# Layer 0 of a four-layer forward pass: row sums of the attention weights spread by transfers instead of a product, and a new written-out order on all engines

## The chip, the cores and the metric

One core of a Trainium2 chip runs the whole program in one launch. The metric is device microseconds from start to end, lower is better. TensorE (PE), VectorE (DVE), ScalarE (ACT), GpSimd (POOL) and SyncE (SP, which here only issues transfers) each run their own list of instructions in order and wait on semaphores for one another.

## The reference

Four layers, each an attention-like branch and a feed-forward branch. Only the first layer is changed. Its two branches are independent up to the end of the part that is spoken of here:

```python
# branch 1: 8 blocks over x of 4 x 512 rows, width 128 (two rows of x share one sum over the sequence)
q, k, v = x @ Wq + bq, x @ Wk + bk, x @ Wv + bv
Q, K = elu(q) + 1, elu(k) + 1
KV, Ksum = (K * v).sum(seq), K.sum(seq)
V = Q * KV / (Q * Ksum + eps)
x = layernorm(gelu(V @ Wo + bo) + x)
x = layernorm(gelu(gelu(x @ Wf1 + bf1) @ Wf2 + bf2) + x)

# branch 2: attention with 16 heads of width 8
scores = q @ k.T / sqrt(8)
attn = softmax(scores)
o = attn @ v
return o @ wo.T + bo      # then norm and a mixture of experts
```

## The kernel before

The function `layer_0_branches` runs both branches at once.

Branch 1 is four streams of 512 columns (`s` = 0 to 3), each through eight blocks `i`. A block of a stream is 16 products of a 128x128 weight with 128x512 data in f32 (`q k v o`, the norm's `n1centre n1var`, `f0` to `f3`, four for `ff`, `n2centre n2var`), with ScalarE, VectorE and GpSimd steps between them. On PE all of them are line L110.

Branch 2 is 16 chunks `m`: half of 1024 queries for a group of four heads. Within a chunk:
- `search` (L498, 16 units of two bf16 products) gives the scores with queries on the rows; VectorE takes row maxima (`maximum`, L708), 2.44 us of it for two units.
- `negate`, `turn` (L507, one transpose on PE), `turn_copy` (L722), and four small transfers on SP (L427, `maxima_rows`) put the negated maxima into an extra row of the query stack.
- `weigh` (L523, 16 units) gives the scores turned, less the maximum; ScalarE takes Exp into `weights` (`weight`, L622).
- `use` (L540, 8 tiles of keys, each four heads side by side on the columns) adds weights times values into one bank, `out`. Row 32j+8 of it is the sum of head j's weights.
- `out` (L629) copies the bank to `mixed`; `sums` (L551, `add_up`) multiplies by the matrix `spread`, which brings row 32j+8 to all 32 rows of head j; `log` and `inverse` (L638, L642) take Ln and then Exp(-x) into the one tile `inv`; `divide` on GpSimd (L744) multiplies `mixed` by it.

The units of `search` and `weigh` share two double banks of PSUM in the order planned (`doubles`); the products of branch 1, `turn` and `sums` share three banks (`singles`). Chunk `m` searches while chunk `m-1` weighs. ScalarE must load another function table whenever it goes from Exp/Ln to Gelu (L566) or back (L561).

The order of the work on each engine is set by `in_order`, which merges the generators by the times that they yield. These times come from a table for one period of 44 units that is repeated 16 times: a time plus `PERIOD` times the chunk's (or block's) number. So the order is the same in each of the inner chunks.

When the last chunk is divided, a barrier of all engines ends the function, and the next one begins with the product of `mixed` with `wout`.

Of the kernel before, what the change touches and what calls it, by code (L numbers as in the profile page):

```python
# [8 lines left out]
ALU = mybir.AluOpType  # L9
ACT = mybir.ActivationFunctionType  # L10
# [217 lines left out]
class Ring:  # L228
# [27 lines left out]
PERIOD = 44.0  # L256
PLAN_ATT = {
    "q": (3.88, 0.80), "k": (-0.00, -3.02), "v": (5.37, 1.59), "exp_k": (0.98, -1.86), "relu_k": (1.52, -0.11),
    "exp_q": (6.24, 2.05), "relu_q": (6.77, 4.58), "less_k": (3.19, -1.17), "K": (4.35, 0.58), "less_q": (13.24, 11.61),
# [4 lines left out]
PLAN_NET = {  # L264
# [5 lines left out]
PLAN_CHUNK = {  # L270
    "search": (10.34, 14.80, 15.01, 18.78, 18.99, 22.65, 22.86, 29.45, 31.73, 36.64, 37.86, 39.71, 42.80, 48.77, 51.26, 54.14),
    "maximum": (12.12, 15.22, 17.08, 19.20, 20.26, 23.42, 24.48, 29.86, 32.17, 37.06, 38.27, 40.77, 43.22, 49.19, 51.67, 54.55),
    "negate": (55.92,), "turn": (59.40,), "turn_copy": (60.83,),
    "weigh": (69.73, 69.93, 72.01, 73.22, 75.52, 76.94, 78.15, 78.36, 80.43, 82.23, 83.50, 86.59, 90.48, 90.68, 92.98, 95.05),
    "weight": (70.77, 71.62, 72.46, 73.92, 75.93, 77.36, 78.57, 79.42, 80.85, 82.71, 84.04, 87.01, 90.89, 91.74, 93.39, 95.46),
    "use": (76.01, 77.23, 80.93, 84.00, 87.09, 90.97, 95.55, 116.29), "out": (117.36,), "sums": (129.64,), "log": (132.28,),
    "inverse": (151.79,)}
# [4 lines left out]
def layer_0_branches(core, w_att, w_f1, w_f2, wa, col, att_landed, cols_landed, q_dram, k_dram, qs, ks, stacks, values, later, mixed):  # L282
# [25 lines left out]
    weights_used, out_copied, sums_ready, logs_done, inv_done, heads_done, values_copied = (  # L308
        sem(n) for n in ("weights_used", "out_copied", "sums_ready", "logs_done", "inv_done", "heads_done", "values_copied"))
    LOADS = 4  # L310

    def att(s, i, name):
        return (2 * i + s // 2) * PERIOD + PLAN_ATT[name][s % 2]

    def net(s, i, name):
        return (2 * i + s // 2 + 1) * PERIOD + PLAN_NET[name][s % 2]

    def chunk(m, name, i=0):
        return m * PERIOD + PLAN_CHUNK[name][i]
# [4 lines left out]
                   [(chunk(m, "turn"), STREAMS + 3, (m, "turn")) for m in range(CHUNKS)] +  # L324
# [6 lines left out]
    def single_free(eng, *key):  # L331
        earlier = singles.earlier(*key)
        if earlier is None:
            return
        if earlier[1] == "turn":
            eng.wait_ge(turned_copied, earlier[0] + 1)
        elif earlier[1] == "sums":
            eng.wait_ge(logs_done, earlier[0] + 1)
        else:
            s, i, name = earlier  # L340
# [3380 lines left out]
```

## Time and profile before

| | |
|---|---|
| median of 3 runs | 1711.33 us (1709.41 to 1718.65) |
| the profiled execution: its time, its span | 1713.21 us, 1711.5 us |
| layer 0's two branches: first product, last division's start | 30.48 us, 819.84 us |
| span 121.2 to 745.6 us: PE busy, ACT busy per 48 us | 48.0, 42.1 us |
| granted TensorE clock over the span | 0.964 |

The span is cut by the 16 transposes of `turn`, which stand 48.04 us apart in the inner chunks. Start times of PE instructions tell more than its durations: the instructions overlap, and what the next one's start leaves is what one costs.

### The profile page before, as it was taken

What the parts mean: (1) busy time and instruction counts of PE and PEld (TensorE: products, weight loads), DVE (VectorE), ACT (ScalarE), POOL (GpSimd) and SP (SyncE); (2) the same over time, 40 slices, a digit from 0 to 9 for tenths busy, and PEclk for the clock granted to TensorE, in tenths of its full rate; (3) what the DMA queues carried; (4) which work ended last, traced back from release to release, by engine and by line L of the source; (5) the groups of instructions that cost most, each with busy time, mean ns of one, the idle gap of its engine ahead of it and who ended that gap; (6) DMA issues with size and microseconds to landing.
All of it is one profiled execution on the core that took longest, in us unless ns stands there. A gap on an engine that the chain in (4) does not pass through costs nothing. (4 is left out here: it accounts for less than half of the span.)

```text
span 1711.5 us, 19967 instructions
## 1 busy us (share of the span) xinstructions
PE 1571.5 (92%) x7054; PEld 682.4 (40%) x7054; DVE 1224.6 (72%) x1736; ACT 1151.8 (67%) x1604; POOL 262.1 (15%) x227
## 2 busy tenths in 40 slices
PE   6999999999999999999799989999877678678998
PEld 3333233333333333332344446665432455333674
DVE  5977777777777777773143325876399889997997
ACT  5688888888888888888333357534475568333663
POOL 1000111111010111111000010000179200582000
PEclk8999999999999999999999988999999889888999
DMA  6200101010010100000252112111353677630000
GB/s 199 57 12 7 25 13 26 13 25 13 7 25 7 25 13 7 13 0 1 60 101 62 37 39 64 46 39 44 99 191 130 204 232 249 177 132 12 1 1 25
DMA packets 66716, 104.18 MB, mean 61 GB/s; under 512 B 9015, under 2 KB 32534, under 8 KB 66596
## 3 DMA queue, kind: packets, MB, share of 16 engines
q1 hardware_dynamic: 55354, 65.15, 14.0%
q10 hardware_dynamic: 9216, 33.56, 6.0%
q0 software_dynamic: 2048, 4.20, 0.8%
q8 instruction: 57, 0.93, 0.2%
q14 instruction: 41, 0.34, 0.1%
HBM read 86.92 MB, written 15.87 MB: 60 GB/s over the span
## 5 line engine op out<-in xcount | busy, mean ns | idle before, releaser
L708 DVE TENSOR_REDUCE best<-quad 128x2 f32<-128x1024 f32 x256 | 309.7, 1221 | 130.5 <-PE quad L498 128.1
L622 ACT ACTIVATE weights<-quad 128x1024 f32<-128x1024 f32 x256 | 255.8, 1029 | 28.6 <-PE quad L523 28.2
L2629 PE MATMUL quad<-l_st,ident 128*128 128x512 f32 x256 | 130.3, 653 | 44.3 <-DVE l_st L2940 44.2
L540 PE MATMUL quad<-weights,values 128*32 128x512 f32 x1024 | 136.4, 605 | 0.4 <-ACT weights L622 0.4
L110 PE MATMUL quad<-q,wf 128*128 128x512 f32 x256 | 121.5, 606 | 0.7 <-DVE q L659 0.3
L110 PE MATMUL quad<-hid,wf 128*128 128x512 f32 x256 | 116.6, 599 | 0.0
L566 ACT ACTIVATE hid<-quad,col 128x512 f32<-128x512 f32 x128 | 84.9, 689 | 21.4 <-PE quad L110 21.2
L734 POOL TENSOR_TENSOR sq_all<-cen_all 128x512 f32<-128x512 f32 x64 | 65.2, 1039 | 213.9 <-DVE cen_all L653 213.9
L110 PE MATMUL quad<-sq_all,mean_w 128*128 128x512 f32 x176 | 94.7, 638 | 1.8 <-ACT sq_all L1367 0.9
L498 PE MATMUL quad<-ks,qs 48*128 48x512 bf16 x512 | 89.5, 385 | 6.8 <-DVE best L708 6.3
L2629 PEld LDWEIGHTS quad<-l_st,ident 128*128 128x128 f32 x256 | 50.7, 209 | 112.3 <-DVE l_st L2940 60.3
L523 PE MATMUL quad<-qs,ks 49*128 49x512 bf16 x512 | 91.5, 384 | 2.2 <-ACT weights L622 2.2
L744 POOL TENSOR_TENSOR mixed<-mixed,inv 128x512 f32<-128x512 f32 x16 | 20.3, 1269 | 465.9 <-ACT inv L642 465.9
L2528 POOL DMA_INDIRECT slots<-l_rows,l_blocks_index x32 | 82.0, 2562 | 42.0 <-ACT l_rows L2746 32.5
L110 PE MATMUL quad<-cur,wa 128*128 128x512 f32 x168 | 87.0, 627 | 0.0
L2923 DVE TENSOR_TENSOR l_st<-l_u,l_bs 128x1024 f32<-128x1024 f32 x64 | 76.5, 1221 | 10.7 <-PE quad L2629 10.7
L523 PEld LDWEIGHTS quad<-qs,ks 49*128 49x128 bf16 x512 | 22.2, 93 | 146.8 <-issue 60.4
L1391 ACT ACTIVATE end_hid<-quad,end_w1s 128x512 f32<-128x512 f32 x64 | 42.9, 688 | 53.5 <-PE quad L110 51.7
L2940 DVE TENSOR_TENSOR l_st<-l_st,l_c_rows 128x1024 f32<-128x1024 f32 x64 | 75.5, 1213 | 0.1
L2931 DVE TENSOR_TENSOR_SCAN l_st<-sq_all,l_st 128x1024 f32<-128x1024 f32 x32 | 71.9, 2276 | 2.2 <-ACT sq_all L2863 2.2
L110 PEld LDWEIGHTS quad<-q,wf 128*128 128x128 f32 x256 | 45.7, 189 | 66.4 <-issue 64.7
L2931 DVE TENSOR_TENSOR_SCAN l_st<-cen_all,l_st 128x1024 f32<-128x1024 f32 x32 | 71.7, 2274 | 0.0
(454 smaller groups left out, 3035.6 us busy)
## 6 DMA issues: line engine op xcount, KB each, us to landing
l_bs<-xd_dram ACTq DMA_DIRECT2D x32, 512.0 KB
l_c_rows<-xd_dram ACTq DMA_DIRECT2D x32, 512.0 KB
end_cs<-comb SPq DMA_DIRECT2D x32, 256.0 KB, 3.9
l_cs<-comb SPq DMA_DIRECT2D x32, 256.0 KB, 3.7
l_weights<-in_F_w SPq DMA_DIRECT2D x30, 257.0 KB, 4.7
wf<-in_L_f SPq DMA_DIRECT2D x16, 256.0 KB, 2.6
l_rows<-in_F_w SPq DMA_DIRECT2D x15, 257.0 KB, 6.0
qs<-q_dram SPq DMA_DIRECT2D x16, 192.0 KB, 3.5
```

Source lines behind the costliest of these rows:

```text
L110: last = nc.tensor.matmul(out[:, c:c + BANK], lhsT, rhs[:, c:c + BANK], start=(n == 0), stop=(n == len(pairs) - 1))
L498: last = nc.tensor.matmul(to[:, par * BANK:(par + 1) * BANK], qs[n % BUFS][rows, slot, qt * P:(qt + 1) * P], ks[n % BUFS][rows, slot, c * ...
L523: last = nc.tensor.matmul(to[:, par * BANK:(par + 1) * BANK], ks[n % BUFS][rows, slot, kt * P:(kt + 1) * P], qs[n % BUFS][rows, slot, c * ...
L540: last = nc.tensor.matmul(out[32 * j:32 * j + 32, :], values[:, kt, GH * g + j, :], weights[p % BUFS][:, j % 2, j // 2, :], start=(kt == 0 ...
L566: return nc.scalar.activation(*args, ACT.Gelu_apprx_tanh, **kwargs)
L622: nc.scalar.activation(weights[p % BUFS][:, slot, :, :].rearrange("p a t -> p (a t)"), doubles.of("weigh", m, i), ACT.Exp, scale=scale).th ...
L708: nc.vector.tensor_reduce(heads[:, :, slot, qt, c], doubles.of("search", m, i).rearrange("p (a t) -> p a t", a=2), AX.X, ALU.max).then_inc ...
L2528: nc.gpsimd.indirect_dma_start(slots_dram, bass.IndirectOffsetOnAxis(blocks.index[:, i, t:t + 1], 0), rows[:, t, :], None).then_inc(scatte ...
L2629: last = nc.tensor.matmul(y[d][:, c:c + BANK], core.ident[:, :], st[n % RING][:, c:c + BANK], start=False, stop=(s == NS - 1), skip_group_ ...
L2923: nc.vector.tensor_tensor(st[n % RING][:, :], u[h][d][:, :], bs[k % 2][:, :], ALU.mult).then_inc(dbx_ready, 1)
L2931: nc.vector.tensor_tensor_scan(out=st[i][:, :], data0=da[i], data1=st[i][:, :], initial=0.0, op0=ALU.mult, op1=ALU.add).then_inc(scanned, 1)
L2940: nc.vector.tensor_tensor(st[n % RING][:, :], st[n % RING][:, :], cs_rows[k % 2][:, :], ALU.mult).then_inc(times_c, 1)
```

## The change

1. `add_up` and the matrix `spread` are gone. In their place SP issues, for each chunk, four transfers (`spread_sums`): row 32j+8 of `mixed` to the 32 rows of head j in `inv`. `log` now reads `inv` and waits for them. Since `inv` is written by the transfers, they wait for the division of the chunk before (`heads_done`); earlier the `log` did.
2. The period table is replaced by `PLAN_0`, which gives for each step of each stream, block and chunk its place in the engine's own order. Nothing repeats any more; the order differs in each chunk. The steps of SP and GpSimd, which were placed by the times of other steps, have places of their own.

```diff
-PERIOD = 44.0
-PLAN_ATT = {
...
+PLAN_0 = {
...
+    "sums": (7, 11, 15, 18, 21, 27, 31, 35, 39, 42, 46, 50, 54, 56, 58, 59,),
+    "load_maxima": (2, 4, 8, 13, 16, 20, 24, 28, 32, 36, 40, 43, 48, 51, 55, 57,),
...
     def att(s, i, name):
-        return (2 * i + s // 2) * PERIOD + PLAN_ATT[name][s % 2]
-
-    def net(s, i, name):
-        return (2 * i + s // 2 + 1) * PERIOD + PLAN_NET[name][s % 2]
+        return at(name, s * B + i)
...
+                def spread_sums():
+                    for m in range(CHUNKS):
+                        yield chunk(m, "sums")
+                        sp.wait_ge(out_copied, m + 1)
+                        if m:
+                            sp.wait_ge(heads_done, m)
+                        for j in range(GH):
+                            row = heads_of(m)[32 * j + HD:32 * j + HD + 1, :]
+                            sp.dma_start(inv[32 * j:32 * j + 32, :],
+                                         row.rearrange("p (a t) -> p a t", a=1).to_broadcast([1, 32, BANK])).then_inc(sums_landed, 16)
...
-                def add_up():
-                    for m in range(CHUNKS):
-                        yield chunk(m, "sums")
-                        if m == 0:
-                            pe.wait_ge(ones_set, 3)
-                        pe.wait_ge(out_copied, m + 1)
-                        single_free(pe, m, "sums")
-                        nc.tensor.matmul(singles.of(m, "sums"), spread[:, :], heads_of(m), start=True, stop=True).then_inc(sums_ready, 1)
...
-                        act.wait_ge(sums_ready, m + 1)
-                        if m:
-                            act.wait_ge(heads_done, m)
-                        nc.scalar.activation(inv[:, :], singles.of(m, "sums"), ACT.Ln).then_inc(logs_done, 1)
+                        act.wait_ge(sums_landed, 16 * GH * (m + 1))
+                        nc.scalar.activation(inv[:, :], inv[:, :], ACT.Ln).then_inc(logs_done, 1)
```

The first place is PE in the middle of an inner chunk (chunk 4 searching). Here `qs,ks` are units of `weigh` (a unit is x2), `ks,qs` units of `search`, `weights,values` tiles of `use` (a tile is x4), and the rest are products of branch 1. Before:

```order
L523 MATMUL quad<-qs,ks 128x512 x2
L498 MATMUL quad<-ks,qs 128x512 x2
L540 MATMUL quad<-weights,values 32x512 x4
L523 MATMUL quad<-qs,ks 128x512 x2
L540 MATMUL quad<-weights,values 32x512 x4
L523 MATMUL quad<-qs,ks 128x512 x4
L110 MATMUL quad<-sq_all,mean_w 128x512 x2
L523 MATMUL quad<-qs,ks 128x512 x2
L498 MATMUL quad<-ks,qs 128x512 x2
L540 MATMUL quad<-weights,values 32x512 x4
L498 MATMUL quad<-ks,qs 128x512 x2
L523 MATMUL quad<-qs,ks 128x512 x2
```

Now, in the same part of a chunk (chunk 5 searching; L660 is `weigh`, L635 `search`, L677 `use`):

```order
L660 MATMUL quad<-qs,ks 128x512 x2
L635 MATMUL quad<-ks,qs 128x512 x2
L677 MATMUL quad<-weights,values 32x512 x4
L660 MATMUL quad<-qs,ks 128x512 x4
L110 MATMUL quad<-sq_all,mean_w 128x512 x2
L635 MATMUL quad<-ks,qs 128x512 x2
L660 MATMUL quad<-qs,ks 128x512 x2
L677 MATMUL quad<-weights,values 32x512 x8
L660 MATMUL quad<-qs,ks 128x512 x2
L635 MATMUL quad<-ks,qs 128x512 x2
L110 MATMUL quad<-cur,wa 128x512
L660 MATMUL quad<-qs,ks 128x512 x2
```

Two tiles of `use` often stand together now (x8); before, each stood alone.

The second place is the end of layer 0 on ScalarE. `weights` is the Exp of a unit, `mixed` the copy of `out`, `inv` Ln or Exp of the sums, `sq_all` the root of branch 1's last norms. Before:

```order
L622 ACTIVATE weights<-quad 128x1024 x4
L573 ACTIVATE sq_all<-quad,eps 128x512
L622 ACTIVATE weights<-quad 128x1024
L577 ACTIVATE sq_all<-sq_all 128x512
L622 ACTIVATE weights<-quad 128x1024 x2
L638 ACTIVATE inv<-quad 128x512
L622 ACTIVATE weights<-quad 128x1024 x4
L642 ACTIVATE inv<-inv 128x512
L629 ACTIVATE mixed<-quad 128x512
L638 ACTIVATE inv<-quad 128x512
L642 ACTIVATE inv<-inv 128x512
```

Now (L750 is `weights`, L757 `mixed`, L764 and L768 Ln and Exp of the sums, L701 and L705 the norms):

```order
L750 ACTIVATE weights<-quad 128x1024 x11
L764 ACTIVATE inv<-inv 128x512
L750 ACTIVATE weights<-quad 128x1024 x2
L768 ACTIVATE inv<-inv 128x512
L757 ACTIVATE mixed<-quad 128x512
L701 ACTIVATE sq_all<-quad,eps 128x512
L705 ACTIVATE sq_all<-sq_all 128x512
L701 ACTIVATE sq_all<-quad,eps 128x512
L705 ACTIVATE sq_all<-sq_all 128x512
L764 ACTIVATE inv<-inv 128x512
L768 ACTIVATE inv<-inv 128x512
```

The roots of the last norms moved from among the last Exps to between the copy of the last chunk and its Ln.

The third place is the end of layer 0 on SP. `wa` and `wf` are weights of the next block, `qs<-negb` the maxima of a chunk. Before:

```order
L392 DMA wa<-in_L_att 128x512
L396 DMA wf<-in_L_f 128x512
L427 DMA qs<-negb 1x4x128 x4
L400 DMA wf<-in_L_f 128x512
L427 DMA qs<-negb 1x4x128 x8
```

Now, with `inv<-mixed` the sums of a chunk:

```order
L564 DMA inv<-mixed 32x1x512 x4
L553 DMA qs<-negb 1x4x128 x4
L564 DMA inv<-mixed 32x1x512 x4
L553 DMA qs<-negb 1x4x128 x4
L564 DMA inv<-mixed 32x1x512 x8
```

Four more transfers a chunk stand in SP's list, each time ahead of a chunk's maxima, and the last eight are the sums of chunks 14 and 15.

## Rows read from the trace of the kernel before

**Rows 1.** The page: busy time of each engine, and PE in 40 equal slices.
```profile
PE 1571.5 (92%) x7054; PEld 682.4 (40%) x7054; DVE 1224.6 (72%) x1736; ACT 1151.8 (67%) x1604; POOL 262.1 (15%) x227
...
PE   6999999999999999999799989999877678678998
```

**Rows 2.** Stretches of layer 0: length; PE, PEld, DVE, ACT, POOL busy (count); clock; DMA.
```profile
30.00:74.00 44.00, 36.15 (x91) 11.82 (x92) 35.57 (x59) 27.07 (x38) 3.48 (x5) 0.84 0.49 138
...
169.20:217.20 48.00, 48.00 (x196) 14.92 (x197) 35.69 (x53) 42.09 (x56) 5.67 (x6) 1.00 0.09 23
...
745.60:788.00 42.40, 42.01 (x179) 13.04 (x178) 30.43 (x37) 36.95 (x47) 7.89 (x7) 1.00 0.00 1
788.00:822.10 34.10, 27.74 (x134) 7.70 (x132) 5.43 (x9) 27.01 (x34) 8.36 (x7) 1.00 0.00 1
```

**Rows 3.** PE's timeline in an inner chunk: start, duration, instruction.
```profile
198.81 0.39 PE L523 MATMUL quad<-qs,ks 49*128 49x512 bf16 x2
199.03 0.38 PE L498 MATMUL quad<-ks,qs 48*128 48x512 bf16 x2
199.34 1.07 PE L540 MATMUL quad<-weights,values 128*32 128x512 f32 x8
200.34 2.84 PE L110 MATMUL quad<-cur,wa 128*128 128x512 f32 x6
203.11 0.60 PE L523 MATMUL quad<-qs,ks 49*128 49x512 bf16 x4
203.65 1.06 PE L540 MATMUL quad<-weights,values 128*32 128x512 f32 x8
204.64 1.12 PE L110 MATMUL quad<-cur,wa 128*128 128x512 f32 x2
...
212.14 4.56 PE L110 MATMUL quad<-q,wf 128*128 128x512 f32 x10
216.63 0.60 PE L498 MATMUL quad<-ks,qs 48*128 48x512 bf16 x4
```

**Rows 4.** The transposes of the maxima: durations, first and last start.
```profile
L507 PE MATMUL quad<-ident,neg x16: 273/277/277, 73.9 to 788.0; 128*16 128x128 f32 x16
```

**Rows 5.** The page: the two readers of the double banks.
```profile
L708 DVE TENSOR_REDUCE best<-quad 128x2 f32<-128x1024 f32 x256 | 309.7, 1221 | 130.5 <-PE quad L498 128.1
L622 ACT ACTIVATE weights<-quad 128x1024 f32<-128x1024 f32 x256 | 255.8, 1029 | 28.6 <-PE quad L523 28.2
```

**Rows 6.** A table load on ScalarE and what follows it, on the timeline.
```profile
788.92 1.28 ACT L561 ACT_TABLE_LOAD   x1
...
790.21 0.63 ACT L642 ACTIVATE inv<-inv 128x512 f32<-128x512 f32 x1
```

**Rows 7.** The timeline from the last tile of `use` to the next function.
```profile
815.56 1.06 PE L540 MATMUL quad<-weights,values 128*32 128x512 f32 x8 [0.45 <-ACT weights L622]
...
816.69 0.60 ACT L629 ACTIVATE mixed<-quad 128x512 f32<-128x512 f32 x1 [0.68 <-PE quad L540]
817.34 0.30 PEld L551 LDWEIGHTS quad<-mixed,spread 128*128 128x128 f32 x2 [1.63 <-ACT mixed L629]
...
818.50 0.60 ACT L638 ACTIVATE inv<-quad 128x512 f32<-128x512 f32 x1 [1.22 <-PE quad L551]
...
819.84 1.26 POOL L744 TENSOR_TENSOR mixed<-mixed,inv 128x512 f32<-128x512 f32 x1 [2.48 <-ACT inv L642]
...
822.13 8.80 PE L110 MATMUL quad<-mixed,wout 128*128 128x512 f32 x16 [3.67 <-PEq L88]
```

**Rows 8.** Transfers on SP: issuing one of the maxima's, and the landing of block weights `wf`.
```profile
L427 SPq DMA_DIRECT2D qs<-negb x64: 572/573/612, 75.9 to 790.5; - x64
...
DMA to landing us min/median/max: 2.5/2.6/4.9
```

**Rows 9.** The start of layer 0: `mix` on VectorE, and the product `o` on PE that waits for it.
```profile
46.46 1.40 DVE L688 SCALAR_TENSOR_TENSOR mq<-q,totals,mk 128x512 f32<-128x512 f32 x2
...
47.25 3.78 PE L110 MATMUL quad<-mq,wa 128*128 128x512 f32 x4
```

More of the change, by code:

```diff
@@ L307, in layer_0_branches, with at @@
     negated, turned, turned_copied, maxima_landed = sem("negated"), sem("turned"), sem("turned_copied"), [sem(f"maxima_landed{i}") for i in range(2)]
[L308 to L309 removed]
+    weights_used, out_copied, sums_landed, logs_done, inv_done, heads_done, values_copied = (
+        sem(n) for n in ("weights_used", "out_copied", "sums_landed", "logs_done", "inv_done", "heads_done", "values_copied"))
     LOADS = 4
+    def at(name, i):
+        return PLAN_0[name][i]
     def att(s, i, name):
[L313 to L316 removed]
+        return at(name, s * B + i)
+    net = att
     def chunk(m, name, i=0):
[L319 removed]
+        return at(name, m * (len(PLAN_0[name]) // CHUNKS) + i)
     bank = [core.quad[b // 4][:, b % 4 * BANK:(b % 4 + 1) * BANK] for b in range(8)]
@@ L323, in layer_0_branches @@
                    [(net(s, i, n), s, (s, i, n)) for s in EVERY for i in range(B) for n in OUTPUTS_NET.split()] +
-                   [(chunk(m, "turn"), STREAMS + 3, (m, "turn")) for m in range(CHUNKS)] +
-                   [(chunk(m, "sums"), STREAMS + 4, (m, "sums")) for m in range(CHUNKS)])
+                   [(chunk(m, "turn"), STREAMS + 3, (m, "turn")) for m in range(CHUNKS)])
     out = bank[3]
@@ L415, in sets @@
                     for n in range(BUFS, len(SETS)):
-                        yield chunk(2 * (n - BUFS) + 1, "use", PAIRS - 1) + 2
+                        yield at("load_set", n - BUFS)
                         sp.wait_ge(weights_used, 2 * PAIRS * (n - BUFS + 1))
@@ L422, in maxima_rows @@
                         n, c = m // 2, m % 2
-                        yield chunk(m, "turn_copy") + 0.5
+                        yield at("load_maxima", m)
                         sp.wait_ge(turned_copied, m + 1)
@@ L542, in use @@
                             last.then_inc(weights_used, 1)
-                def add_up():
-                    for m in range(CHUNKS):
-                        yield chunk(m, "sums")
-                        if m == 0:
-                            pe.wait_ge(ones_set, 3)
-                        pe.wait_ge(out_copied, m + 1)
-                        single_free(pe, m, "sums")
-                        nc.tensor.matmul(singles.of(m, "sums"), spread[:, :], heads_of(m), start=True, stop=True).then_inc(sums_ready, 1)
-                in_order(*(stream(s) for s in EVERY), search(), weigh(), use(), turn_maxima(), add_up())
+                in_order(*(stream(s) for s in EVERY), search(), weigh(), use(), turn_maxima())
             @block.scalar
@@ L741, in divide @@
                     for m in range(CHUNKS):
-                        yield chunk(m, "inverse") + 1
+                        yield at("divide", m)
                         pool.wait_ge(inv_done, m + 1)
@@ L747, in second_values @@
                     for g in range(GROUPS):
-                        yield chunk(2 * g + 1, "use", PAIRS - 1) + 3
+                        yield at("second", g)
                         pool.wait_ge(weights_used, 2 * PAIRS * (g + 1))
```

139 lines of the change are left out of this document (114 added, 25 removed), and 47 rows, old and new, of tables (PLAN_0, PLAN_ATT, PLAN_NET).

## The prediction

> **What bounds the kernel now.** I read the page first: TensorE is busy 92% of the span, and its row of slices shows nines through the part in which layer 0 runs [rows 1]. Next the stretches: in an inner chunk PE is busy 48.00 of 48.00 us, ScalarE 42.1, VectorE 35.7 [rows 2]. Busy is modelled for PE, so I went to its timeline, where the starts give prices. The 16 transposes of the maxima run from 73.9 to 788.0 us [rows 4]; inner chunks repeat every 48.04 us. If the starts are explained by work alone, layer 0 is as long as PE's list is.
>
> The prices, from starts [rows 3]:
> - A 128x128 product (two instructions): six instructions take 2.77 us (200.34 to 203.11), ten take 4.49 (212.14 to 216.63). Two more products cost 1.72, so one costs 0.86, and 0.19 is left over once per run of products.
> - A unit of search or weigh: 0.22 (198.81 to 199.03). Two and then something else: 0.54 (203.11 to 203.65), so 0.10 is left over once per run.
> - A tile of `use` and then something else: 0.99 (203.65 to 204.64). Two tiles together are nowhere in the trace. The tile streams the same two rounds as a product, so the part paid once per run lies between 0 and 0.13; I take 0.10, as for the units.
>
> An inner chunk then is 33 products (28.4), 13 runs of them (2.5), 32 units (7.1), 17 runs of them (1.7), eight lone tiles (8.0), a transpose (0.1): 47.8 of 48.04 us. PE waits for nearly nothing there: layer 0 is bound by PE's list from the first transpose to the last. Two ends are different. Ahead of the first transpose PE is busy 36 of 44 us at a lower clock; after the last one it is busy 27.7 of 34.1 and ScalarE 27.0 [rows 2], and there the Exps set the pace.
>
> **The change, part by part.** Counts are from the orders of the two programs.
>
> *The sums' products.* 14 of the 16 stand ahead of the last transpose: 14 x 0.86 = -12.0 us. The other two stand in the part that ScalarE paces, one of them in the last chain.
>
> *The runs.* Ahead of the last transpose PE had 203 runs of products, 263 of units, 119 of tiles; it has 192, 261 and 77, since tiles stand in pairs. 11 x 0.19 + 2 x 0.10 + 42 x 0.10 = -6.5 us (with the tile's price at 0 it is -2.3, at 0.13 -7.8).
>
> *Steps moved.* Three more products of branch 1 (-2.6 us) now stand behind the last transpose. There PE has 15 instead of 14, two sums' less included, and six runs fewer, in 6.4 us of PE idleness [rows 2], so they are free.
>
> *The start.* The product `o` starts at 47.25, as soon as `mix` begins to deliver at 46.46 [rows 9]. Five reductions of 1.22 us [rows 5] stood ahead of `mix` on VectorE; two do now. It is worth 3.6 us if nothing else held `mix`, and 0 if VectorE's 35.6 busy us of 44 [rows 2] just come in another order. I take -1.
>
> *Table loads.* ScalarE loads 73 tables instead of 67, as three runs of Gelu are split. One is 1.28 us, with the next instruction right behind it (788.92, then 790.21) [rows 6], so 7.7 us over the layer. ScalarE idles 5.9 us per 48 [rows 2]; the cover is about 85 us, and I cost them at 0. Without cover they cost all 7.7. The Trainium skill (ScalarE: Activation LUTs, What ACT_TABLE_LOAD costs) gives 1283 ns for the load, as here, but adds some 1380 ns of drain to each switch; by it ScalarE would lose 16 us. The row shows no such gap.
>
> *New waits.* Units leave PE faster than readers empty the two double banks: a reduction takes 1.22 us, an Exp 1.03 [rows 5]. Before, one order that left 0.24 us of waits was repeated; now each chunk is another. Units of `weigh` follow each other in pairs 75 times (50 before), and a pair needs 2.06 us of ScalarE. If each of 25 more pairs lost some 0.1 us, and three or four late Lns behind the transfers 0.5 us each, it is 4 us. Bounds: 0, and 10 (0.7 a chunk). I take +4.
>
> *The transfers inside the layer.* The chain of chunk m's sums (copy, four transfers, Ln, Exp, division) has a chunk's length until `out` is copied again. SP is in order: behind the four issues stand the next maxima. The last maxima transfer of a chunk is issued 2.5 us after the transpose (790.5 against 788.0) [rows 4, 8], landing 2.5 us later at the least [rows 8]: 5.0 us. PE has 10.4 us of products and units between transpose and first `weigh` unit before; now never under 8.2, and 6.0 in the last chunk. With the sums' own four issues of 0.57 us ahead it still fits. Cost 0.
>
> *The end.* Before, the copy of `out` ends at 817.29, Ln starts at 818.50: 1.21 us for the product. After: four issues, the last started after 3 x 0.57 = 1.7 us, and its landing 2.5 us on [rows 7, 8]: 4.2 us, so +3.0. The division of chunk 14 ahead of it ends with the copy, as now, +0.2. Bounds: short issues of 0.2 and a landing of 2.0 would give +1.4, the longest landing of 4.9 [rows 8] +5.5. In this gap lie the four instructions of the last norms (2.7 us), their VectorE steps and two additions on GpSimd; the division comes after these in GpSimd's list, and they end at about the time of the Exp. I take +3.2. The Trainium skill (DMA: Bandwidth & Descriptors, Anatomy of one DMA) puts some 2.0 us of fixed cost on any transfer, which speaks against moving a 0.86 us product to one; by it the end would cost +2.6. The stretch from last transpose to last tile, 27.6 us [rows 4, 7], holds the same 16 Exps and three tables, so 0.
>
> Sum: -12.0 - 6.5 - 2.6 - 1 + 4 + 3.2 = -14.9 us. The profiled execution took 1713.2, so 1698.3; it lies 1.9 over the median of the runs, 1711.3, against which that is 1696.4. I say 1696. Beyond layer 0 nothing changes.
>
> **Rivals.**
> 1. *The new order's waits eat it.* PE has no reserve, but the readers and streams have only some: ScalarE at 88% would be at 91 to 93% with a shorter chunk and more tables. If ScalarE's late Exps cost PE 0.7 us a chunk (10 us in place of 4) and the end costs 5.5, the gain is 6 to 7: 1704 to 1705. For it: 7.7 us more work on the second-busiest engine, unequal chunks. Against: 5.9 us of idleness in every chunk.
> 2. *The start gains fully, nothing waits.* -3.6 at the start and +1 of waits, tiles at 0.13: -22, 1689. For it: the list on PE is a sum of fixed prices. Against: no order is without waits.
> 3. *Slower.* SP's single queue: `inv` is one tile, so the sums of chunk m wait for the division of m-1, and the maxima behind them wait too. The Exp for it stands 1 to 33 instructions ahead of the copy of chunk m on ScalarE, in three chunks under five. It decides once that division is later than the next transpose by the cover's remainder, 8.2 - 5.0 - 2.3 = 0.9 us in the tightest chunk; each us beyond stops PE. To lose the 14.9 and 8.6 more, 23.5 us, 15 chunks must lose 1.6 each, so 1722 or more. Against: from copy to the next transpose there is over half a chunk (some 50 of 67 PE steps).
> 4. *The product's removal alone counts.* If runs cost nothing that PE has to pay (an overlap of the drains with waits that are there anyway): 6.5 less, 1703.
>
> **How the numbers follow.** Forecast (all terms within 4 us) 0.55; rival 1 0.16; rival 2 0.12; rival 4 0.10; rival 3 or another loss 0.07. The measurement tells 0.5%, 8.6 us, from no change: faster means under 1702.8. The forecast and rival 2 lie there, and of the 0.26 around rivals 1 and 4, which lie just beyond the bound, somewhat under half: 0.55 + 0.12 + 0.11 = 0.78. Within 0.5%: the rest of 1 and 4, 0.15. Slower 0.07. The range reaches to both faster rivals and to the near edge of the slow one's: 1687 to 1709. The likeliest case alone is 1692 to 1701.
>
> **What the profile after would show.** The transposes end near 769 to 771 instead of 788.0, that is 46.3 to 46.5 us apart on average. PE stays at nine tenths or more through the layer; its starts show two tiles of `use` at 1.85 to 1.98 us. ScalarE is busy about 0.5 us a chunk more, and Lns on `inv` seldom have a wait on transfers ahead. From copy of the last chunk to its Ln about 4.4 us. Wrong would be: PE idle rows in inner chunks that end by ScalarE or VectorE, of over 0.7 us a chunk (rival 1); maxima transfers issued late after `turn_copy` (rival 3); a lower granted clock in the layer, which would raise every price and which I have no reason to expect while PE stays busy.

## The result, and the profile after

The change made the kernel about 1% slower: 1733.2 us median of nine runs against 1717.1 us for the kernel before, measured beside it in as many runs. The ratio is 1.0097, 95% interval 1.0077 to 1.0118. The forecast was 1696 us, about 1% faster. The profiled execution took 1729.2 us (span 1727.5), 16.0 more than the one of before. The page after, with the lines that answer to [rows 1], the granted clock, and the row of the queue that carries SP's transfers:

```profile
PE 1564.9 (91%) x7022; PEld 682.4 (40%) x7022; DVE 1237.7 (72%) x1736; ACT 1157.6 (67%) x1610; POOL 271.5 (16%) x225
...
PE   6999998999999999999699989999986688677998
...
PEclk8999999999999999999899989999899899888999
...
q1 hardware_dynamic: 58426, 69.35, 18.5%
```

TensorE does have less to do, but 6.6 us less only, and an eight stands among the nines of the layer (the seventh slice, 259 to 302 us): it is not full all through any more. Stretches of the layer after, with the columns of [rows 2]:

```profile
30.00:71.00 41.00, 35.15 (x91) 11.34 (x92) 34.64 (x55) 26.35 (x38) 2.92 (x3) 0.88 0.53 148
164.60:211.20 46.60, 46.56 (x186) 14.81 (x185) 36.09 (x53) 42.05 (x56) 6.25 (x6) 1.00 0.21 29
260.45:310.60 50.15, 45.72 (x181) 14.27 (x180) 32.98 (x50) 39.73 (x53) 6.11 (x6) 0.93 0.18 27
455.70:511.70 56.00, 52.76 (x206) 16.45 (x205) 40.69 (x55) 45.00 (x59) 7.37 (x7) 0.97 0.15 24
...
798.00:836.00 38.00, 28.08 (x136) 8.18 (x134) 6.22 (x9) 29.00 (x36) 8.43 (x7) 0.95 0.29 15
```

One inner chunk (164.60) is what was forecast: 46.60 us, full. The chunk at 260.45 lost 4.4 us to idleness, the one at 455.70 lost 3.2, and in both the granted clock is below one, which it never was between the first and the last transpose before. The last stretch, 34.1 us before [rows 2], is longer too. The transposes of the maxima, as in [rows 4]:

```profile
L644 PE MATMUL quad<-ident,neg x16: 270/273/277, 70.9 to 798.0; 128*16 128x128 f32 x16
```

The start gave 3.0 us, the stretch from first to last transpose took 12.9 more (727.0 against 714.1), the end 7.4 more (34.1, then 41.5: `wout` starts at 839.51, against 822.13 in [rows 7]). Together 17.4, and the rest of the kernel gave back the small remainder to the span's 16.0.

What took the place of the removed work shows in the timeline of the changed kernel around chunk 3:

```profile
275.38 0.60 ACT L757 ACTIVATE mixed<-quad 128x512 f32<-128x512 f32 x1
...
277.21 1.26 POOL L870 TENSOR_TENSOR mixed<-mixed,inv 128x512 f32<-128x512 f32 x1
...
278.55 3.18 SPq L564 DMA_DIRECT2D inv<-mixed  x4
...
286.03 0.39 PE L660 MATMUL quad<-qs,ks 49*128 49x512 bf16 x2
...
287.89 0.63 ACT L764 ACTIVATE inv<-inv 128x512 f32<-128x512 f32 x1 [4.47 <-DMA inv<-mixed]
...
289.67 1.92 ACT L750 ACTIVATE weights<-quad 128x1024 f32<-128x1024 f32 x2
290.72 0.10 PEld L635 LDWEIGHTS quad<-ks,qs 48*128 48x128 bf16 x2 [4.60 <-ACT weights L750]
290.73 0.61 PE L635 MATMUL quad<-ks,qs 48*128 48x512 bf16 x2 [4.31 <-ACT weights L750]
```

Read it upwards. TensorE stood still for over 4 us, because a bank had not been read by an Exp (L750). The Exp stood in ScalarE's list behind the Ln of the sums (L764), and that waited 4.47 us for the transfers of `inv`. The copy ends at 275.98, but the four issues start only at 278.55: `inv` is one tile, and they wait for the division of chunk 2, which ends at 278.47. The Ln runs at 287.89. The view of the tile `inv` counts these waits and gives the landing:

```profile
its engine sat idle before it (us, times) until:
...
  DMA inv<-mixed: 16.3, 4
...
DMA to landing us min/median/max: 4.6/5.7/8.3
```

Three of the four are in the layer (chunks 3, 7 and 9), the fourth is at its end. A stop of TensorE has a second price. Here are the stretches around the stop of chunk 3 and at the end:

```profile
286.00:289.50 3.50, 0.42 (x6) 0.10 (x2) 0.00 (x0) 1.58 (x3) 0.00 (x0) 0.99 0.76 206
289.50:296.30 6.80, 5.57 (x11) 1.77 (x12) 3.60 (x4) 4.84 (x7) 0.00 (x0) 0.50 0.01 5
296.30:300.00 3.70, 3.70 (x21) 0.95 (x23) 2.07 (x2) 3.13 (x5) 0.00 (x0) 1.00 0.00 0
836.00:839.50 3.50, 0.00 (x0) 0.02 (x1) 0.00 (x0) 1.11 (x2) 1.27 (x2) 0.50 0.00 0
```

After 3.5 us in which TensorE did almost nothing, its granted clock was 0.50, the lower of its two levels, for 6.8 us, then 1.00 again. The lower level came back with the waits of chunks 7 and 9, 3.4 us each.

And the end, in the timeline, against [rows 7]:

```profile
825.97 0.60 ACT L757 ACTIVATE mixed<-quad 128x512 f32<-128x512 f32 x1 [0.67 <-PE quad L677]
...
826.72 3.10 SPq L564 DMA_DIRECT2D inv<-mixed  x4
...
829.73 1.70 POOL L864 TENSOR_TENSOR x<-x,cur 128x512 f32<-128x512 f32 x1 [3.08 <-DVE cur L785]
...
831.78 1.26 POOL L864 TENSOR_TENSOR x<-x,cur 128x512 f32<-128x512 f32 x1 [0.36 <-DVE cur L785]
835.85 0.63 ACT L764 ACTIVATE inv<-inv 128x512 f32<-128x512 f32 x1 [6.28 <-DMA inv<-mixed]
836.51 0.63 ACT L768 ACTIVATE inv<-inv 128x512 f32<-128x512 f32 x1
837.22 1.26 POOL L870 TENSOR_TENSOR mixed<-mixed,inv 128x512 f32<-128x512 f32 x1 [4.17 <-ACT inv L768]
839.51 8.52 PE L110 MATMUL quad<-mixed,wout 128*128 128x512 f32 x16 [11.70 <-PEq L88]
```

From the end of the copy (826.57) to the Ln 9.3 us pass, where before 1.2 did, and the norms that stand between fill little of it: the Ln waits 6.28.

### The profile page after: what moved, and what is told of

Its sections match the earlier page's. It is cut to its first block and busy times, and to the rows that moved or that the text cites. A ratio compares the mean times of both kernels' runs of the same rounds, so it can differ in the third digit from the quotient of the medians.

```text
span 1727.5 us, 19954 instructions
## 1 busy us (share of the span) xinstructions
PE 1564.9 (91%) x7022; PEld 682.4 (40%) x7022; DVE 1237.7 (72%) x1736; ACT 1157.6 (67%) x1610; POOL 271.5 (16%) x225
## 3 DMA queue, kind: packets, MB, share of 16 engines
q1 hardware_dynamic: 58426, 69.35, 18.5%
q0 software_dynamic: 2048, 4.20, 0.8%
## 5 line engine op out<-in xcount | busy, mean ns | idle before, releaser
L750 ACT ACTIVATE weights<-quad 128x1024 f32<-128x1024 f32 x256 | 253.4, 1026 | 29.9 <-PE quad L660 26.0
L860 POOL TENSOR_TENSOR sq_all<-cen_all 128x512 f32<-128x512 f32 x64 | 69.5, 1099 | 431.0 <-DVE cen_all L779 430.9
L677 PE MATMUL quad<-weights,values 128*32 128x512 f32 x1024 | 129.2, 605 | 0.1
L660 PE MATMUL quad<-qs,ks 49*128 49x512 bf16 x512 | 93.9, 388 | 11.5 <-ACT weights L750 7.1
L635 PE MATMUL quad<-ks,qs 48*128 48x512 bf16 x512 | 90.2, 387 | 10.3 <-DVE best L834 4.9
L2648 POOL DMA_INDIRECT slots<-l_rows,l_blocks_index x32 | 86.4, 2701 | 44.3 <-ACT l_rows L2866 34.9
L660 PEld LDWEIGHTS quad<-qs,ks 49*128 49x128 bf16 x512 | 22.3, 93 | 148.7 <-ACT weights L750 88.5
L110 PEld LDWEIGHTS quad<-hid,wf 128*128 128x128 f32 x256 | 46.4, 190 | 58.0 <-issue 58.0
L782 DVE TENSOR_TENSOR cen_all<-cen_all,sq_all 128x512 f32<-128x512 f32 x64 | 44.7, 701 | 33.2 <-ACT sq_all L705 33.2
```

Of the source, the lines that this page charges most:

```text
L110: last = nc.tensor.matmul(out[:, c:c + BANK], lhsT, rhs[:, c:c + BANK], start=(n == 0), stop=(n == len(pairs) - 1))
L635: last = nc.tensor.matmul(to[:, par * BANK:(par + 1) * BANK], qs[n % BUFS][rows, slot, qt * P:(qt + 1) * P], ks[n % BUFS][rows, slot, c * ...
L660: last = nc.tensor.matmul(to[:, par * BANK:(par + 1) * BANK], ks[n % BUFS][rows, slot, kt * P:(kt + 1) * P], qs[n % BUFS][rows, slot, c * ...
L677: last = nc.tensor.matmul(out[32 * j:32 * j + 32, :], values[:, kt, GH * g + j, :], weights[p % BUFS][:, j % 2, j // 2, :], start=(kt == 0 ...
L750: nc.scalar.activation(weights[p % BUFS][:, slot, :, :].rearrange("p a t -> p (a t)"), doubles.of("weigh", m, i), ACT.Exp, scale=scale).th ...
L2648: nc.gpsimd.indirect_dma_start(slots_dram, bass.IndirectOffsetOnAxis(blocks.index[:, i, t:t + 1], 0), rows[:, t, :], None).then_inc(scatte ...
```

## How the numbers of all kernels are put together

For every kernel the starts of TensorE between first and last transpose are read from the timeline one by one. From each distance between two starts the smallest one that the same pair of kinds of instruction has anywhere in that stretch is taken away; the sum of what is left over is called the **excess** (waits and time at the lower clock). The stretch less the excess is the **list**: an estimate of what the instructions would take if nothing waited. "wout" is the start of the product behind the layer. Times in us; the last column is the ratio to the kernel before with its interval.

| kernel | first transpose | last | excess | list | wout | ratio |
|---|---|---|---|---|---|---|
| before | 73.9 | 788.0 | 7.4 | 706.7 | 822.1 | 1 |
| after | 70.9 | 798.0 | 40.5 | 686.5 | 839.5 | 1.0097 (1.0077 to 1.0118) |
| old_transfers | 73.5 | 776.0 | 8.1 | 694.4 | 818.2 | 0.9990 (0.9968 to 1.0011) |
| old_transfers_14 | 74.5 | 777.0 | 8.0 | 694.5 | 811.1 | 0.9911 (0.9880 to 0.9941) |
| old_paired | 74.0 | 821.9 | 49.9 | 698.0 | 857.4 | 1.0165 (1.0122 to 1.0209) |
| new_product | 70.3 | 837.1 | 68.2 | 698.6 | 881.1 | 1.0354 (1.0312 to 1.0397) |
| new_late_ln | 70.4 | 784.5 | 27.6 | 686.5 | 826.0 | 1.0022 (0.9999 to 1.0044) |
| new_late_ln_last_product | 70.5 | 784.7 | 27.7 | 686.5 | 822.0 | 0.9974 (0.9946 to 1.0002) |
| new_many_rows | 71.6 | 785.1 | 27.1 | 686.4 | 822.5 | 0.9989 (0.9958 to 1.0019) |
| new_one_transfer | 71.3 | 789.5 | 31.8 | 686.4 | 828.9 | 1.0048 (1.0021 to 1.0074) |
| new_short_max | 69.9 | 771.6 | 16.3 | 685.4 | 813.2 | one execution |
| new_short_exp | 72.5 | 778.2 | 20.0 | 685.7 | 816.7 | one execution |
| old_short_max | 68.4 | 770.9 | 8.4 | 694.1 | 813.1 | one execution |
| old_short_exp | 73.8 | 771.5 | 3.8 | 693.9 | 810.3 | one execution |

The places are those of one profiled execution of each kernel. From `wout` on all kernels run the same code, and yet that part took between 883.8 us (new_late_ln_last_product) and 901.2 us (old_transfers_14), so a gain of a few us is judged by the ratio.

How a stretch is split into list and excess depends on how finely the kinds are told apart. With nothing but products, units, tiles and transposes as kinds, the list of after is 24.3 us shorter than that of before, and new_late_ln has 23.4 us more of excess than before; in the table these are 20.2 and 20.2. By prices, the list between first and last transpose should be 20.6 shorter: 17 products fewer at 0.86, four runs of products at 0.19, two of units at 0.10, and 42 runs of tiles at 0.12. So read these figures as good to some 3 us. The ends of the stretches do not depend on it.

## The experiments

**old_transfers: the transfers alone, in the old order.** The product leaves the kernel before; everything else stays where it was.

```diff
+    "sums_out": (118.0,)
...
+    def spread_sums():
+        for m in range(CHUNKS):
+            yield chunk(m, "sums_out")
...
-                in_order(block_weights(), sets(), maxima_rows())
+                in_order(block_weights(), sets(), maxima_rows(), spread_sums())
...
-                        nc.scalar.activation(inv[:, :], singles.of(m, "sums"), ACT.Ln).then_inc(logs_done, 1)
+                        act.wait_ge(sums_landed, 16 * GH * (m + 1))
+                        nc.scalar.activation(inv[:, :], inv[:, :], ACT.Ln).then_inc(logs_done, 1)
```

> The order of the kernel before, with the four one-row transfers in place of the sums' product in all chunks. If the loss comes from where the changed plan puts its Lns (theory 1: the transfers need some 9.3 us from the copy to the Ln, and only short covers and the end pay for it), this order covers them, since the repeated order's Ln stands about 17 us behind the copy: 14 products of 0.86 us less, 8 us more at the end, so 4 us faster than before, ratio 0.998. If the transfers hurt by themselves (theory 2: they load SP's queue, the DMA engines or the SBUF wherever they stand), waits appear in every chunk and it is slower than before, ratio 1.005 or more.

The transposes end at 776.0, 12.0 us earlier, with the excess where it was (8.1). The transposes in the view of the tile `neg`:

```profile
L517 PE MATMUL quad<-ident,neg x16: 272/277/277, 73.5 to 776.0; 128*16 128x128 f32 x16
```

And the end in the timeline:

```profile
804.64 0.60 ACT L630 ACTIVATE mixed<-quad 128x512 f32<-128x512 f32 x1 [0.67 <-PE quad L550]
805.39 3.10 SPq L437 DMA_DIRECT2D inv<-mixed  x4
...
814.52 0.63 ACT L637 ACTIVATE inv<-inv 128x512 f32<-128x512 f32 x1 [9.28 <-DMA inv<-mixed]
```

So 14 products are worth their price, 14 x 0.86, and in the old order the transfers are hidden inside the layer. At its end they are not: from the end of the copy (805.24) to the Ln 9.3 us, as in the changed kernel. That gives back 8.1 of the 12, and the ratio can't be told from one.

**new_product: the new order alone, with the product.** The product stands just ahead of each Ln's place in TensorE's plan.

```diff
+    "sums_pe": (177.5, 243.5, 309.5, 337.5, 444.5, 511.5, 542.5, 606.5, 712.5, 742.5, 814.5, 913.5, 953.5, 1039.5, 1062.5, 1080.5),
```

> The changed kernel's order, with the sums' product put back on TensorE just ahead of each Ln, and no transfers. Theory 3 (the order that doesn't repeat leaves 1 to 2.7 us of small waits in each chunk, 17 us in all, whatever makes the sums) says: 12 us of products come back, three stalls of 10 us, 7 us of halved clock and 8 us at the end go, so 13 us faster than the changed kernel, about level with before or slightly slower, ratio 1.000 to 1.004. If the transfers alone make the loss, the order itself is worth its fewer runs and shorter start: 8 to 10 us faster than before, ratio 0.994 to 0.995.

It was far slower, 68.2 us of excess. The run says little about the order: the product holds one of the three single banks until its Ln, and ScalarE's `mk` then waited 56.6 us for products whose bank was late. TensorE itself stood still for 37 us, most of it until a Ln had freed a bank. I count the run as inconclusive for the order, and its expectation as missed; only its list (698.6, that is 12.1 over the changed kernel's) repeats the price of 14 products.

**new_late_ln: the three Lns that waited, moved back on ScalarE.**

```diff
-    "log": (133, 184, 234, 255, 336, 388, 414, 460, 544, 565, 621, 697, 726, 787, 806, 815,),
+    "log": (133, 184, 234, 272.5, 336, 388, 414, 472.5, 544, 580.5, 621, 697, 726, 787, 806, 815),
```

> The changed kernel with the Lns of chunks 3, 7 and 9 put 12 to 17 places later in ScalarE's order; nothing else. Theory 1: the three waits of ScalarE for the transfers (4.5, 2.8 and 2.7 us of TensorE idleness) and the halved clock behind them go, 10 to 17 us faster than the changed kernel, ratio to before 1.000 to 1.004. If they only uncover other waits, it stays at 1.007 or more.

The transposes end 13.5 us earlier (view of `neg`), and only the wait at the end is left (view of `inv`):

```profile
L644 PE MATMUL quad<-ident,neg x16: 269/273/278, 70.4 to 784.5; 128*16 128x128 f32 x16
```

```profile
  DMA inv<-mixed: 6.3, 1
```

The excess falls by 12.9 (40.5 to 27.6). TensorE's three stops account for 9.7 of it (4.3, 2.7 and 2.7). The rest fits the lower clock behind them: between the transposes it was granted for 13.7 us in the changed kernel and for 3.4 us here. No run prices it by itself. But 27.6 is still 20.2 more than before: the late Lns were the smaller part.

**new_many_rows: the same bytes, read from 32 partitions.** Each transfer takes 32 rows of `mixed` in place of one row 32 times; Ln reads a constant, so the sums do not enter the output.

```diff
-                            row = heads_of(m)[32 * j + HD:32 * j + HD + 1, :]
+                            row = heads_of(m)[32 * j:32 * j + 32, :]
...
-                        nc.scalar.activation(inv[:, :], inv[:, :], ACT.Ln).then_inc(logs_done, 1)
+                        nc.scalar.activation(inv[:, :], inv[:, :], ACT.Ln, scale=0.0, bias=core.one[:, :]).then_inc(logs_done, 1)
```

> The changed kernel, but each of the four transfers of a chunk takes the head's own 32 rows instead of one row 32 times, and the Ln multiplies what it reads by 0 and adds 1, so the sums are left out of the result. Same bytes, same packets, same order. If reading one partition 128 times is what makes the packets slow (0.69 us for 2 KB where a weight's packet takes 0.08), a transfer lands in 2 to 3 us, no Ln waits, and it is 17 us faster than the changed kernel plus 4 or 5 at the end: ratio to before 0.998 to 1.001. If the time is a fixed cost of a transfer, landing stays at 5 us or more and the time does too.

The view of `inv`:

```profile
  DMA inv<-mixed: 1.0, 1
...
DMA to landing us min/median/max: 1.9/2.0/4.5
```

The end in the timeline:

```profile
814.52 1.86 SPq L564 DMA_DIRECT2D inv<-mixed  x3
...
817.84 0.72 ACT L764 ACTIVATE inv<-inv,one 128x512 f32<-128x512 f32 x1 [1.01 <-DMA inv<-mixed]
```

The landing falls from 5.7 to 2.0 us, and with it all four waits but 1.0 us. The places of the Lns are those of the changed kernel, so the other half of the fault is shown: the places were too early only because one row was read 32 times. The pages of the profiles say the same in other units. Queue q1 holds the same 58426 packets and 69.35 MB in both, but takes 18.5% of 16 engines' time in the changed kernel and 14.8% here, against 14.0% before with 3072 packets less. So the 3072 added packets (2048 of 2 KB, the others small) cost 5113 - 3834 = 1279 us of engine time (0.42 us a packet on average) from one row, and 234 us (0.08 a packet) from 32.

The Trainium skill (SBUF — State Buffer, Door 1: The DMA port swizzle) says that a transfer's rate depends on how many of 16 ports its partitions reach, 27.2 GB/s a port, and by its table partitions 8 and 40 share one port, and 72 and 104 another. So the four rows lie on two ports, each gives 128 KB, and an estimate from that page is 4.8 us for the four. The Trainium skill (DMA: Bandwidth & Descriptors, Anatomy of one DMA) gives 2.0 us of fixed cost, in a section on transfers issued by GpSimd, while these are issued by SP; with it the estimate is 6.8. The run that fits this estimate best is the next one, where one issue takes all four rows: 6.9 us. With four issues it was 9.1 us from the first issue's start (826.72) to the Ln at the end of the changed kernel, and 7.4 from the last one's (828.5). Transfers from 32 partitions landed in 2.0, about that page's fixed cost. No run here tells a slow port from a slow single partition: new_many_rows changes both.

**new_one_transfer: four issues made one.**

```diff
-                        for j in range(GH):
...
+                        row = heads_of(m)[HD::32, :]
+                        sp.dma_start(inv[:, :],
+                                     row.rearrange("p (a t) -> p a t", a=1).to_broadcast([GH, 32, BANK])).then_inc(sums_landed, 16)
...
-                        act.wait_ge(sums_landed, 16 * GH * (m + 1))
+                        act.wait_ge(sums_landed, 16 * (m + 1))
```

> The changed kernel, with one transfer for the sums of a chunk in place of four (four rows, each 32 times, same bytes). Three issues of 0.64 us go. If the 128 packets of 2 KB read their partitions as slowly as now (0.69 us each), the copy-to-Ln time falls only by the issues, from 9.3 to 7 or 8 us, the Lns of chunks 3, 7 and 9 still wait, and it gains 5 us on the changed kernel (ratio to before 1.005 to 1.007). If the four partitions are read side by side, it falls to 4 us, no Ln waits, and the ratio is 0.998 to 1.001.

The end in the timeline:

```profile
818.30 0.56 SPq L563 DMA_DIRECT2D inv<-mixed  x1
...
825.23 0.63 ACT L763 ACTIVATE inv<-inv 128x512 f32<-128x512 f32 x1 [4.08 <-DMA inv<-mixed]
```

From the issue to the Ln 6.9 us remain. Issuing four times was 1.8 us of the chain (826.72 to 828.5 in the changed kernel); the transfer itself is the rest. In the layer two waits of the Ln are left, 3.6 us together, and the kernel is still slower than before, as expected.

**old_transfers_14 and new_late_ln_last_product: the last chunk by the product.** All other sums go by transfers. The edit is shown for the old order, against old_transfers.

```diff
-                    for m in range(CHUNKS):
+                    for m in range(15):
...
+                    for m in range(15, CHUNKS):
+                        yield chunk(m, "sums")
```

> The order of before with transfers for the first 15 chunks and the product for the last one, so that no transfer stands in the chain to the next function. Theory 1: the last transpose comes 12 us earlier, as with transfers in all chunks (776.0 against 788.0), and the end is as long as before (34 us), so 12 us faster than before, ratio 0.993. A rival would be that the clock or the later functions take it back: 0.997 or more.

> The changed order with the three Lns later, and the product for the last chunk alone. The end shortens by the 7 us of the transfers, so the next function starts at 819 instead of 826: 3 us faster than before, ratio 0.998; with old_transfers_14 it shows what the order alone costs when every transfer is covered: theory 3 says some 8 us to the last transpose (784.5 against 776.0). If the order were worth its fewer runs, it would be the faster of the two.

The end of old_transfers_14 in its timeline:

```profile
806.36 1.10 PE L562 MATMUL quad<-mixed,spread 128*128 128x512 f32 x2 [0.76 <-issue]
807.49 0.60 ACT L651 ACTIVATE inv<-quad 128x512 f32<-128x512 f32 x1 [1.23 <-PE quad L562]
...
811.11 10.08 PE L110 MATMUL quad<-mixed,wout 128*128 128x512 f32 x16 [3.65 <-PEq L88]
```

In the old order the end is as short as before (777.0 to 811.1, 34.1 us), the gain of 11 us is kept, and the ratio is 0.9911: 1704.7 us median, faster than both kernels. In the new order the same step gives 4 us at wout, and 0.9974, which can't be told from one. The transfers are the same in these two, and the difference between them is the order: +7.7 us at the last transpose, although its list is 8.0 shorter.

**old_paired: tiles of `use` in pairs, in the kernel before.** Runs of tiles fall from 119 to 74, those of units from 263 to 232.

```diff
-    "use": (76.01, 77.23, 80.93, 84.00, 87.09, 90.97, 95.55, 116.29), ...
+    "use": (77.22, 77.23, 83.99, 84.00, 90.96, 90.97, 95.55, 116.29), ...
```

> The kernel before with one change of its table: the tiles of use are planned in pairs (three of the four pairs of a chunk), sums still by the product. Ahead of the last transpose TensorE's runs of tiles fall from 119 to 74 and its runs of units from 263 to 232. If a run costs what I took for it (0.10 us each), the list is 7.6 us shorter; if nothing waits for it, 7.6 us faster, ratio 0.996. Theory 3 says that waits take part of it: with three weights buffers ScalarE's Exp of the tile after next waits for the pair, so 1 to 3 us of waits a chunk may come, and it is no faster or slower (1.00 to 1.02).

TensorE's timeline at a pair of tiles:

```profile
292.08 0.38 PE L498 MATMUL quad<-ks,qs 48*128 48x512 bf16 x2
293.42 0.39 PE L523 MATMUL quad<-qs,ks 49*128 49x512 bf16 x2 [0.96 <-ACT weights L622]
293.74 1.92 PE L540 MATMUL quad<-weights,values 128*32 128x512 f32 x16
295.60 0.61 PE L523 MATMUL quad<-qs,ks 49*128 49x512 bf16 x4
```

Two tiles take 1.86 us (293.74 to 295.60) where two lone ones take 1.98, so a run of tiles costs 0.12. By that and 0.10 for a run of units the list should be 8.5 shorter, and it is 8.7. Yet the kernel lost 34 us at the last transpose, because a pair needs two units' Exps at once and TensorE waited for them in every chunk, twice 0.96 us in an inner one: 42.5 us more of excess. That is what an order costs that is good for TensorE and bad for its readers.

**new_short_max, new_short_exp: who makes the new order wait.** Both are new_late_ln. The first reduces 256 of 1024 columns in each maximum of the search (0.42 us), the second takes the Exp of 256 of 1024 columns (0.38 us), with the other weights fixed at 1.

```diff
-   nc.vector.tensor_reduce(heads[:, :, slot, qt, c], doubles.of("search", m, i).rearrange("p (a t) -> p a t", a=2),
+   nc.vector.tensor_reduce(heads[:, :, slot, qt, c], doubles.of("search", m, i).rearrange("p (a t) -> p a t", a=2)[:, :, 0:128],
...
-   nc.scalar.activation(weights[p % BUFS][:, slot, :, :].rearrange("p a t -> p (a t)"), doubles.of("weigh", m, i),
+   nc.scalar.activation(weights[p % BUFS][:, slot, 0, 0:256], doubles.of("weigh", m, i)[:, 0:256],
```

> The changed order with late Lns, but VectorE's row maxima read a quarter of the columns (three quarters are left out), so a reduction takes some 0.35 us instead of 1.22. If the 27 us of small waits on TensorE between first and last transpose are VectorE's lateness (its queue or its reading of the double banks), they fall below 12; if they are ScalarE's, they stay above 20.

> The changed order with late Lns, but ScalarE's Exp takes a quarter of each unit (256 of 1024 columns; the rest of the weights stays at 1). The other half of the question on the small waits, 27.6 us on TensorE: with VectorE's reductions shortened they were 16.3. If ScalarE's reading of the double banks and its lateness for the streams make the rest, they fall to 15 or below here, and TensorE's waits ahead of units of weigh nearly vanish; if they are the streams' own chains, they stay near 20.

**old_short_max, old_short_exp: the same two edits on old_transfers.**

> The repeated order with transfers (old_transfers), VectorE's maxima over a quarter of the columns (three quarters left out). It gives the floor for new_short_max: TensorE's waits between first and last transpose are 8.1 us in old_transfers, and if they are all the double banks' readers, they fall to 2 to 5 here. Then the changed order still has 11 or more us of waits beyond it with VectorE shortened (16.3), and had 19.5 beyond it with VectorE at full length: the difference is what VectorE adds in the changed order alone.

> The repeated order with transfers, ScalarE's Exp over a quarter of each unit (the rest of the weights stays at 1). The floor for new_short_exp: 8.1 us of waits fall to 3 to 6 if ScalarE's reading makes half of them; the changed order had 20.0 with it shortened and 27.6 without.

In the new order light maxima take 11.3 us of the excess away (27.6 to 16.3), light Exps 7.6 (to 20.0). In the old order light maxima take nothing (8.1, then 8.4) and light Exps 4.3 (to 3.8). I had expected old_short_max to fall, too: a miss. For new_short_max I had set under 12 for VectorE and over 20 for ScalarE, and 16.3 is neither. For new_short_exp I had set 15 or below for ScalarE and near 20 for the chains of branch 1's streams, and it was 20.0. So the 20.2 us that the new order adds are not one reader's fault. VectorE's maxima have a hand in 11.3 of them, and did not before; ScalarE's Exps in 3.3 more than before; some 5.6 are left that neither edit takes. This sum takes the two effects as independent, and no run lightens both readers at once; each of the four is one execution.

Part of VectorE's share can be seen. Rows of new_late_ln's timeline, the stretch behind them with the columns of [rows 2], and its groups by form between 75 and 770 us (busy, mean ns, idle before):

```profile
604.82 1.31 POOL L870 TENSOR_TENSOR mixed<-mixed,inv 128x512 f32<-128x512 f32 x1 [35.26 <-ACT inv L768]
604.93 1.75 DVE L822 TENSOR_TENSOR k<-mk,q 128x512 f32<-128x512 f32 x1
...
607.97 0.39 PE L660 MATMUL quad<-qs,ks 49*128 49x512 bf16 x2 [0.89 <-DVE best L834]
```

```profile
609.60:613.00 3.40, 3.40 (x5) 1.37 (x5) 0.65 (x2) 1.55 (x2) 0.00 (x0) 0.50 0.00 0
```

```profile
L860 POOL TENSOR_TENSOR sq_all<-cen_all 128x512 f32<-128x512 f32 x60 | 65.4, 1104 | 403.8 <-DVE cen_all L779 403.7
...
L818 DVE TENSOR_TENSOR k<-mk,cur 128x512 f32<-128x512 f32 x28 | 22.3, 803 | 5.1 <-ACT mk L694 5.1
```

VectorE's addition of two tiles takes 0.69 us at most places and 1.75 here, where it started 0.11 us after GpSimd's division. Before, the same addition `k<-mk,cur` took 683 ns in the mean and GpSimd's squares 1039; now 803 and 1104. Between 75 and 770 us none of VectorE's 117 additions of two tiles met an operation of GpSimd before; in new_late_ln 16 do. In the six where VectorE began first, its addition took 0.68 us as always; in the ten where GpSimd was at work already, it took 0.79 to 1.76. By the Trainium skill (SBUF — State Buffer, SBUF: two separate sides) an operation of VectorE with two such inputs and one of GpSimd take turns at a shared pair of ports, the later one blocked; the rows agree. On VectorE, which is not full, this is small: 28 x 0.12 = 3.4 us in that group. But its maxima come later by it. Behind the meeting at 604.82 TensorE stopped for 0.89 and 0.65 us until maxima were done, and then ran 3.4 us at the lower clock. With light maxima neither these stops nor that spell are there; with light Exps the stops stay and the spell is gone. So in the 11.3 and in the 7.6 there is some lower clock, too.

## Why the prediction was wrong, by its own steps

- *The sums' products, -12.0:* right. old_transfers moved the last transpose by 12.0.
- *The runs, -6.5, and the steps moved, -2.6:* right. The list fell by 20.2 (20 to 24, by how it is counted) where the three terms make 21.1; old_paired confirms the price of runs.
- *The start, -1:* mis-sized, it was -3.0 at the first transpose. `o` starts 3.9 us earlier (43.38 against 47.25), 0.5 of which is that the whole layer starts earlier (29.93 against 30.48). So `mix` gained nearly all of the 3.6 us that the prediction gave as the most. The lower clock has a part in it: between 20 and 60 us it was granted for 13.7 us, against 17.1 before.
- *Table loads, 0:* not tested by itself. ScalarE was busy 42.05 of 46.60 us in a full chunk, so it still had some idle time there; but if the loads made its Exps late, that is part of the 20.2 us below.
- *The transfers inside the layer, 0:* **failed**, worth +12.9. Two things were wrong in it. I took "a chunk's length" as cover, which holds for the reuse of `out`, not for the Ln, whose place in ScalarE's list is the chain's real deadline; in chunks 3, 7 and 9 that place came some 7.5 us behind the copy, and 4.5, 3.2 and 2.4 us too early. And I read the landing from the transfer of `wf`, 2.5 us [rows 8], which reads many rows, while one row read 32 times took 5.7, and the last of four 7.4 from its issue, so 9.1 us and more from the copy. A third thing made it worse: the issues of chunk 3 began 2.6 us after the copy's end, since they waited for the division of chunk 2, and those of chunk 7 began 1.6 us after it, behind other issues in SP's list. That is 4.2 of the 10.0 us that the three Lns waited. new_late_ln and new_many_rows each take one half away (the place, the landing), and either alone is enough: the last transpose comes at 784.5 and 785.1. The prediction had allowed for three or four late Lns, at 0.5 us each, in its term of new waits; there were three, and they waited 2.4 to 4.5 us.
- *A lower granted clock, which I had no reason to expect:* wrong as a consequence of that. With stops of 2.7 to 4.3 us came 3.4 to 6.8 us at the lower level.
- *New waits, +4 (bounds 0 to 10):* **mis-sized**, and the largest miss of the sum: +20.2 with the late Lns removed (new_late_ln against before). I had counted the pairs of `weigh` units and given each a tenth of a us, and gave `search` and VectorE nothing; more than half of it hangs on VectorE's maxima. The bound of 0.7 us a chunk had no row behind it: the only order in the trace was one that waited for nothing, and from such an order no price of another one can be read.
- *The end, +3.2 (bounds to +5.5):* **mis-sized**, +7.4. From the copy's end to the Ln 4.2 us were forecast and 9.3 measured, again by the landing.

Of the rivals, the first named the right mechanism for the larger half, ScalarE's and VectorE's lateness, but let it cost 10 us at most. The third gave the right size, 1722 and over, with another mechanism. The view of waits on SP's queue, between 70 and 800 us, shows that its premise held and its consequence did not:

```profile
SPq L553 <- DVE negb L848: 380.3, 15, 33.5
SPq L561 <- POOL mixed L870: 70.0, 10, 13.7
```

The transfers did wait for the division of the chunk before (L561, ten times), but the queue then still stood idle for 380 us until maxima were there (L553), 15 times in all, so the maxima were not what was sent late. What was late by that wait were the sums' own transfers, as in chunk 3.

The sum, read anew: -20.2 (list) - 3.0 (start) + 20.2 (waits of the new order) + 12.9 (transfers inside the layer) + 7.4 (end) = +17.3, measured +17.4 at the start of `wout`. It had to close, since its terms are differences of the table above; what the runs test is which edit moves which term.

What stays open: which places of the new order cost the 20.2 us one by one, and whether an order as short as the new one exists in which the readers keep up. The 5.6 us that neither light maxima nor light Exps take were not traced. That the order makes the 20.2 us is shown (the same transfers in the old order cost 8.1 us of excess and not 27.6); how much each reader has in them is shown only roughly.

## What to carry to other kernels

When a transfer takes the place of work on the bounding engine, look for its first reader's place in the list of the engine that reads it and measure the shortest distance from source to there, over every repetition, against the landing of a transfer *of the same source shape*. A list that is shorter for the full engine is no gain while two others at 75 to 90% must keep step with it: only the order that had been repeated with almost no waits kept the product's 12 us. Mix the two ways: transfers where a chunk of other work covers them, the product where the chain is bare, gave 0.9911.

## What the runs showed of the hardware

- Transfers that read one partition 32 times cost 0.42 us of engine time a packet against 0.08 from 32 partitions, and landed in 5.7 us against 2.0 (medians).
- Three stops of TensorE of 2.7 to 4.3 us each came with 3.4 to 6.8 us at granted clock 0.50, and with the stops 12.9 us of excess went, where the stops themselves were 9.7. Shorter stops came with it once and not another time: in new_late_ln 3.4 us at 0.50 stood behind stops of 0.89 and 0.65 us; in the changed kernel and in new_short_exp the same two stops had none; and in old_paired, with two stops of 0.96 us in every inner chunk, the clock stayed at 1.00 between the transposes.
- When an addition of two tiles on VectorE met an operation of GpSimd, the one that began later was lengthened: VectorE's took up to 1.75 us instead of 0.69, and GpSimd's squares up to 1.50 instead of 1.04.
- The last of a chunk's four one-row transfers landed 7.2 to 8.3 us after its issue in the changed kernel, the first of the four 4.6 to 5.0.
